# Compact recurrent weights on row halves, and the expert squares on ScalarE, in a one-core TTT, attention and mixture-of-experts kernel

## The reference

```python
def step(carry, xi):                      # per chunk of 128 tokens, 4 heads of 64
    W0, W1, W2, M0, M1, M2 = carry
    qi, ki, vi, l0, l1, l2, mi = xi
    hid = einsum('bcd,bhd->bch', qi, W2)
    gate = silu(einsum('bcd,bhd->bch', qi, W0))
    out = einsum('bch,boh->bco', gate * hid, W1)
    gba = einsum('bcd,bhd->bch', ki, W0)
    hbm = einsum('bcd,bhd->bch', ki, W2)
    sg = silu(gba)
    hidden = sg * hbm
    dhidden = einsum('bco,boh->bch', vi, W1)
    dhbm = dhidden * sg
    dgba = _silu_bp(dhidden * hbm, gba)
    dw1 = einsum('bco,bch->boh', vi, hidden * l1)
    dw0 = einsum('bch,bcd->bhd', dgba, ki * l0)
    dw2 = einsum('bch,bcd->bhd', dhbm, ki * l2)
    ...                                   # momentum, then five Newton-Schulz steps on each
    return (renorm(W0 + dw0, n0), renorm(W1 + dw1, n1), renorm(W2 + dw2, n2), M0n, M1n, M2n), out

# routed experts, 32 of them, latent size 128, weights cw per token
h = square(relu(einsum('tl,eil->eti', x_lat, w1)))
y_lat = einsum('eti,eli->tl', h * cw.T[:, :, None], w2)
```

## Time and profile before

| | |
|---|---|
| median of 3 runs | 830.14 us (828.5 to 830.5) |
| the profiled execution | 830.14 us, of which the span from first to last instruction is 828.1 us |
| TensorE busy | 780.7 us |
| VectorE busy | 714.6 us |
| GpSimd busy | 406.8 us |
| ScalarE busy | 354.0 us |
| relus of the experts on ScalarE | 128, 594 ns each |
| squares of the experts on GpSimd | 128, 1071 ns each |

### The profile page before, as it was taken

One profiled execution on the slowest core, in us unless ns is written; L12 is line 12 of the kernel. 1 busy time (PEld: TensorE's weight loads), 2 busy tenths in 40 slices (PEclk: granted clock), 3 DMA queues, 4 the chain that ended last, 5 costly groups with the idle time before them and its releaser, 6 DMA issues.

```text
span 828.1 us, 24889 instructions
## 1 busy us (share of the span) xinstructions
PE 780.7 (94%) x9776; PEld 668.5 (81%) x9776; DVE 714.6 (86%) x2592; ACT 354.0 (43%) x868; POOL 406.8 (49%) x535
## 2 busy tenths in 40 slices
PE   3899999999999999999999999999999999999997
PEld 1888888888888888878888788887888888888886
DVE  4789898898988979889798897988979889898876
ACT  2544344443444434444344444444444444434533
POOL 1654555445454454544555445544465444655442
PEclk9899999999999999999999999999999999999999
DMA  8100000000000000000000000000000000000000
GB/s 321 54 3 14 9 2 21 3 13 9 2 21 2 14 8 2 21 2 15 8 3 20 2 15 9 3 21 2 15 8 2 21 2 15 8 2 15 2 15 7
DMA packets 9811, 15.09 MB, mean 18 GB/s; under 512 B 1120, under 2 KB 8928, under 8 KB 9440
## 3 DMA queue, kind: packets, MB, share of 16 engines
q1 hardware_dynamic: 7904, 7.80, 3.2%
q10 hardware_dynamic: 1792, 5.70, 1.8%
HBM read 11.41 MB, written 2.10 MB: 16 GB/s over the span
## 4 chain that ended last, share of the span: by engine, by line
PE 53%; DVE 33%; issue 6%; ACT 5%; POOL 2%; DMA 1%; SPq 0%; DVEq 0%
PE CC L629 18%; PE M L629 13%; PE HB L629 8%; DVE acc L1328 8%; PE YB L629 8%; DVE Wn L1175 4%; DVE Mp L1138 2%; DVE dhb L1094 2%; DVE X L1146 2%; PE CC L699 2%; DVE Am L1131 2%; POOL r L285 2%; DVE sm L1233 1%; DMA rows<-in_rows 1%; PE CC L700 1%
## 5 line engine op out<-in xcount | busy, mean ns | idle before, releaser
L363 POOL TENSOR_TENSOR hq<-hr 128x512 f32<-128x512 f32 x128 | 137.1, 1071 | 71.9 <-ACT hr L426 71.9
L285 POOL TENSOR_TENSOR r<-r,half 128x3 f32<-128x3 f32 (+1 forms) x78 | 77.9, 1011 | 155.1 <-DVE r L1116 67.9
L629 PE MATMUL HB<-xlT,e_s 128*128 128x128 f32 x1024 | 143.0, 283 | 0.4 <-ACT xlT L426 0.4
L629 PE MATMUL YB<-e_s,hq 128*128 128x128 f32 x1024 | 141.3, 281 | 1.8 <-DVE acc L1328 0.8
L629 PEld LDWEIGHTS HB<-xlT,e_s 128*128 128x128 f32 x1024 | 126.7, 193 | 6.8 <-ACT xlT L426 0.7
L1328 DVE SCALAR_TENSOR_TENSOR acc<-YB,cw,acc 128x128 f32<-128x128 f32 x448 | 125.4, 342 | 7.9 <-PE YB L629 7.9
L341 POOL TENSOR_TENSOR aX<-X,a_tile 128x192 f32<-128x192 f32 x150 | 92.9, 640 | 79.9 <-DVE X L1146 79.9
L426 ACT ACTIVATE hr<-HB 128x512 f32<-128x512 f32 x128 | 76.1, 594 | 128.5 <-PE HB L629 128.5
L629 PEld LDWEIGHTS YB<-e_s,hq 128*128 128x128 f32 x1024 | 124.2, 191 | 7.4 <-issue 4.1
L629 PEld LDWEIGHTS CC<-X,Mp 64*64 64x64 f32 x1800 | 58.3, 135 | 23.6 <-issue 11.3
L629 PEld LDWEIGHTS CC<-Am 64*64 64x64 f32 x1800 | 59.5, 134 | 21.8 <-DVE Am L1131 18.2
(11 more groups left out here) (180 smaller groups left out, 1525.3 us busy)
## 6 DMA issues: line engine op xcount, KB each, us to landing
xa<-in_x SPq DMA_DIRECT2D x16, 128.0 KB, 2.1
e_s<-in_e1T ACTq DMA_DIRECT2D x1, 2048.0 KB, 12.7
e_s<-in_e2T ACTq DMA_DIRECT2D x1, 2048.0 KB, 19.3
xr<-in_x SPq DMA_DIRECT2D x16, 128.0 KB, 2.2
out<-ot SPq DMA_DIRECT2D x16, 128.0 KB, 1.7
wall<-in_wall SPq DMA_DIRECT2D x1, 820.0 KB, 7.1
up_s<-in_upT ACTq DMA_DIRECT2D x1, 512.0 KB, 15.9
down_s<-in_downT ACTq DMA_DIRECT2D x1, 512.0 KB, 20.0
```

What stands on the lines that cost most here:

```text
L285: return pool.tensor_tensor(dst, src, expo[:, 0:n], ALU.pow)
L363: pool.tensor_tensor(hq[b][:, :, :], hr[b][:, :, :], hr[b][:, :, :], ALU.mult).then_inc(e_hq, 1)
L629: return pe.matmul(out_, lhsT, rhs, start=start, stop=stop)
```

## The change

Two things are changed together. The squares of the experts' rows move from GpSimd (`h_sq`, removed) into `h_relu` on ScalarE; the wait for `y_down(i, u-2)` moves with them and stands ahead of the Relu. The turned weights WT become compact, [128, 3, 64], with head h on partitions 64h to 64h+63: `turn_w` makes them by products with a 64x64 identity on the diagonal quarters, `w_T` copies them by one instruction, `k_side` and `q_side` work on one row half of the array per head, and the k side of head 0 goes to bank CA, that of head 1 to CB. A block-diagonal WO of the third turned weight, for `q_out`, is copied by VectorE in `w_out` behind the k side, in place of W1BD behind `renorm`.

```diff
-            def h_sq(i, u):
-                pool.wait_ge(e_hr, NU * i + u + 1)
-                if u > 1 or not (isinstance(i, int) and i == 0):
-                    pool.wait_ge(e_y, NU * i + u - 1)
-                b = u % 2
-                pool.tensor_tensor(hq[b][:, :, :], hr[b][:, :, :], hr[b][:, :, :], ALU.mult).then_inc(e_hq, 1)
...
             def k_side(i, g):
                 act.wait_ge(e_k[g], i + 1)
-                a(ks[g][:, 0, :], CB[g][:, 0:P], ACT.Sigmoid)
-                a(ks[g][:, 1:3, :].rearrange("p w c -> p (w c)"), CB[g][:, P:3 * P], ACT.Copy).then_inc(e_kc[g], 1)
+                a(ks[g][:, 0, :].rearrange("p (h c) -> p h c", h=2), KS[g][:, :, 0:HD], ACT.Sigmoid)
+                a(ks[g][:, 1:3, :].rearrange("p w (h c) -> p h w c", h=2),
+                  KS[g][:, :, HD:3 * HD].rearrange("p h (w c) -> p h w c", w=2), ACT.Copy).then_inc(e_kc[g], 1)
...
             def w_T(m, g):
 
                 act.wait_ge(e_wt[g], m + 1)
-                for h in range(2):
-                    c = slice(h * HD, (h + 1) * HD)
-                    ins = a(WT[g][c, :, c], CA[g][0:HD, 0:3 * P].rearrange("p (w c) -> p w c", w=3)[:, :, c], ACT.Copy)
-                ins.then_inc(e_WT[g], 1)
+                a(WT[g][:, :, :].rearrange("p w c -> p (w c)"), CA[g][:, 0:3 * HD], ACT.Copy).then_inc(e_WT[g], 1)
...
                 act.wait_ge(e_h, NU * i + u + 1)
                 if u > 1 or not (isinstance(i, int) and i == 0):
                     act.wait_ge(e_hq, NU * i + u - 1)
-                a(hr[u % 2][:, :, :].rearrange("p s t -> p (s t)"), HB[:, :], ACT.Relu).then_inc(e_hr, 1)
+                    act.wait_ge(e_y, NU * i + u - 1)
+                flat = "p s t -> p (s t)"
+                a(hr[u % 2][:, :, :].rearrange(flat), HB[:, :], ACT.Relu).then_inc(e_hr, 1)
+                act.wait_ge(e_hr, NU * i + u + 1)
+                a(hq[u % 2][:, :, :].rearrange(flat), hr[u % 2][:, :, :].rearrange(flat), ACT.Square).then_inc(e_hq, 1)
...
                 pe.wait_ge(e_WT[g], i + 1)
-                mm(CB[g][:, 0:2 * P], qkT[:, 2 + g, :], WT[g][:, W0:W2 + 1, :].rearrange("p w c -> p (w c)"))
-                pe.wait_ge(e_bd[g], i + 1)
-                mm(CB[g][:, 2 * P:3 * P], vT[:, g, :], W1BD[g][:, :]).then_inc(e_k[g], 1)
+                halves = [(slice(h * HD, (h + 1) * HD), (CA, CB)[h][g]) for h in range(2)]
+                for c, dst in halves:
+                    mm(dst[:, 0:2 * HD], qkT[c, 2 + g, :], WT[g][c, W0:W2 + 1, :].rearrange("p w c -> p (w c)"))
+                for c, dst in halves:
+                    ins = mm(dst[:, 2 * HD:3 * HD], vT[c, g, :], Wn[g][c, W1, :])
+                ins.then_inc(e_k[g], 1)
...
                 for w in range(3):
-                    ins = pe.transpose(CA[g][0:HD, w * P:(w + 1) * P], Wn[g][:, w, :], ident[:, :])
+                    for h in range(2):
+                        c = slice(h * HD, (h + 1) * HD)
+                        ins = mm(CA[g][c, w * HD:(w + 1) * HD], Wn[g][c, w, :], ident[c, c])
                 ins.then_inc(e_wt[g], 1)
...
                     for n, w in enumerate((W0, W2)):
-                        ins = mm(M0[:, (2 * g + n) * P:(2 * g + n + 1) * P], WT[g][:, w, :], qkT[:, g, :])
+                        for h in range(2):
+                            c = slice(h * HD, (h + 1) * HD)
+                            ins = mm(M0[c, (2 * g + n) * P:(2 * g + n + 1) * P], WT[g][c, w, :], qkT[c, g, :])
                 ins.then_inc(e_qs, 1)
...
                 for g in range(G):
-                    ins = mm(M1[:, g * P:(g + 1) * P], gh[:, g, :], WT[g][:, W1, :])
+                    pe.wait_ge(e_wo[g], i + 1)
+                    ins = mm(M1[:, g * P:(g + 1) * P], gh[:, g, :], WO[g][:, :])
                 ins.then_inc(e_qo, 1)
...
+            def w_out(i):
+
+                for g in range(G):
+                    dve.wait_ge(e_WT[g], i + 1)
+                    nc.vector.tensor_copy(WO[g][0:HD, 0:HD], WT[g][0:HD, W1, :])
+                    nc.vector.tensor_copy(WO[g][HD:P, HD:P], WT[g][HD:P, W1, :]).then_inc(e_wo[g], 1)
...
                 k_side(i)
+                w_out(i)
                 q_gate(i)
```

More of the change, by code:

```diff
@@ L110, in build @@
         Wn = [sb(f"Wn{g}", [P, 3, HD]) for g in range(G)]
-        W1BD = [sb(f"W1BD{g}", [P, P]) for g in range(G)]
-        WT = [sb(f"WT{g}", [P, 3, P]) for g in range(G)]
+        WT = [sb(f"WT{g}", [P, 3, HD]) for g in range(G)]
+        WO = [sb(f"WO{g}", [P, P]) for g in range(G)]
         Mom = [sb(f"Mom{g}", [P, 3, HD]) for g in range(G)]
@@ L199, in build @@
         CB = [CC[g][:, 512:1024] for g in range(G)]
+        KS = [CC[g][:, :].rearrange("p (h c) -> p h c", h=2)[:, :, 0:3 * HD] for g in range(G)]
         M0 = bank("M0")
@@ L223, in build @@
         e_prod, e_mp = (per_group(n) for n in ("product", "Mp"))
-        e_up, e_rn, e_rp, e_wn, e_bd, e_wt, e_WT = (per_group(n) for n in ("upd", "rn", "rp", "Wn", "W1BD", "wt", "WT"))
+        e_up, e_rn, e_rp, e_wn, e_wo, e_wt, e_WT = (per_group(n) for n in ("upd", "rn", "rp", "Wn", "WO", "wt", "WT"))
         e_qs, e_gsig, e_gt1, e_gh, e_qo, e_to = (sem(n) for n in ("q_side", "gate_sig", "gt1", "gh", "q_out", "to_copied"))
@@ L356, in shared_sq @@
                 pool.tensor_tensor(us[:, :, :], ur[:, :, :], ur[:, :, :], ALU.mult).then_inc(e_us, 1)
-            def h_sq(i, u):
-                pool.wait_ge(e_hr, NU * i + u + 1)
-                if u > 1 or not (isinstance(i, int) and i == 0):
-                    pool.wait_ge(e_y, NU * i + u - 1)
-                b = u % 2
-                pool.tensor_tensor(hq[b][:, :, :], hr[b][:, :, :], hr[b][:, :, :], ALU.mult).then_inc(e_hq, 1)
             def body(i, last):
                 if last:
-                    h_sq(i, 1)
-                    h_sq(i, 2)
                     shared_sq(i)
-                    h_sq(i, 3)
                     rms_pow(i)
-                    for u in range(4, NU):
-                        h_sq(i, u)
                     return
@@ L382, in body @@
                 prep_rstd(m)
[L383 to L386, removed]
+                fill = {0: [lambda: shared_sq(i)], 3: [lambda: rms_pow(i)],
+                        9: [lambda: prep_n8(m)], 16: [lambda: window(m, first)],
                         17: [lambda: prep_kl(m)]}
@@ L397, in body @@
                     row_pow(m, g)
-                h_sq(m, 0)
             prep_rstd(0)
@@ L405, in _ @@
             prep_kl(0)
-            h_sq(0, 0)
             body(0, False)
@@ L978, in _ @@
                 nc.vector.memset(Mom[g][:, :, :], 0.0)
-                nc.vector.memset(W1BD[g][:, :], 0.0)
-                nc.vector.memset(WT[g][:, :, :], 0.0)
+                nc.vector.memset(WO[g][:, :], 0.0)
             nc.vector.memset(lt[:, :, :], 0.0).then_inc(e_init, 1)
@@ L1074, in silu @@
                     dve.wait_ge(e_kc[g], i + 1)
-                    tt(kt[g][:, 0, :], CB[g][:, 0:P], sg[g], ALU.mult).then_inc(e_kd[g], 1)
+                    tt(kt[g][:, 0, :].rearrange("p (h c) -> p h c", h=2), KS[g][:, :, 0:HD],
+                       sg[g].rearrange("p (h c) -> p h c", h=2), ALU.mult).then_inc(e_kd[g], 1)
                 def slope(g):
@@ L1177, in renorm @@
                     ins.then_inc(e_wn[g], 1)
-            def w_bd(m):
+            def w_out(i):
                 for g in range(G):
[L1182 to L1187, removed]
+                    dve.wait_ge(e_WT[g], i + 1)
+                    nc.vector.tensor_copy(WO[g][0:HD, 0:HD], WT[g][0:HD, W1, :])
+                    nc.vector.tensor_copy(WO[g][HD:P, HD:P], WT[g][HD:P, W1, :]).then_inc(e_wo[g], 1)
             def q_gate(i):
@@ L1388, in body @@
                 renorm(m)
-                w_bd(m)
                 total(i)
@@ L1401, in _ @@
                 nc.vector.tensor_copy(nrm[g][:, :], r3[g][:, 4, :]).then_inc(e_up[g], 2)
-            w_bd(0)
             dve.wait_ge(e_const, 16 * NCONST)
```

## The result

The changed kernel takes 930.09 us (928.43 to 930.32), the kernel before 830.32 us beside it: a ratio of 1.120, 95% interval 1.118 to 1.122. It is 100 us slower, 24 us more than the 906 us of the forecast and just inside its range of 875 to 931 us. The profiled execution has a span of 927.9 us.

What follows compares the result with a forecast made beforehand. TensorE, 94% busy, bounds the kernel, under 2.1 us per tile to win. 5.38 - 0.3 - 0.1 = 5.0 us over 15 tiles is 75, plus 0.5 to 1 ahead of tile 0, on 828.1: about 904, plus 2.0 outside the span: 906 us, range 875 to 931.

Steps and rivals of the forecast that it cites:

- Part 1: Squares on ScalarE, their wait on the expert matmul two units back ahead of the Relu: costs 5.38 us per tile.
- The steps: Stalls from the Relu's wait at units 3 to 6: +1.47, +1.90, +1.63 (then +0.30 at a later YB), +0.49 us.
- the +0.08: At unit 5, the XT matmuls behind the sgs matmul come another 0.08 us later.
- step a): Unit 3: Relu waits for YB, then Square and XT copy; first XT matmul 1.47 us later.
- 0.49 given back: The unit 6 stall is taken in by 0.51 us idle before the X,Mp matmuls, where VectorE is late: -0.49 us.
- stall d): Unit 6: Relu, Square, table load, lt and XT copy in a row; XT matmuls 0.49 us later.
- the clock: Rival: each tile has one stretch of 7 us at half speed, 53 us in all, 959 us; chance 7%.
- Part 2: GpSimd no longer holds dhb (0.7 us of TensorE's waits), Wn (0.5) and one lt operation (0.1), per tile.
- Part 3: Compact weights, from Wn to the moments: cost 0.9 us per tile on TensorE, from +0.3 to +2.3.
- overlapping end: Row halves of the array work at once: q side 0.90 us, k side 0.33 per group, +0.3 us in sum.
- The faster one: Rival: waits on e_y already met, squares cost some 0.8 us per tile against 2.1 of old waits; 810 us; chance 4%.
- half hidden: Rival: other old slack takes in the unit 4 or unit 5 stall, 3 us per tile, 875 us; chance 7%.

Runs made afterwards that it cites:

- e5: The changed kernel with matmuls that nobody reads put into TensorE's three long stalls; 906.6 us, ratio 1.0918.
- e1: The changed kernel with four hq buffers instead of two, the Relu waiting for the expert matmul four units back; 828.75 us, ratio 0.9974.
- e7: The changed kernel with four hq buffers, only the Relu of unit 4 still waiting two units back; 865.83 us, ratio 1.0429.
- e8: The changed kernel with four hq buffers, only the Relu of unit 3 still waiting two units back; 848.27 us, ratio 1.0210.
- e4: The kernel before with the squares on ScalarE and four hq buffers, weights as before; 824.48 us, ratio 0.9926.
- e10: The kernel before with the experts' squares left out, YB fed by the Relu from four hr buffers; 799.06 us, ratio 0.9612.
- e12: e11 with compact weights, the WO copies moved behind the reduction of the moments and the two sum copies; 804.3 us, ratio 0.9685.
- e11: e4 with the squares of units 3, 5 and 1 behind the copies that TensorE waits for; 801.43 us, ratio 0.9641.
- e9: The changed kernel, two hq buffers, with the wait on e_y between Relu and Square instead of ahead of the Relu; 868.0 us, ratio 1.0436.

## Why the prediction was right, and what it missed

**Part 1, the wait ahead of the Relu**, was the point, and right in mechanism, place and size. The steps forecast 1.47, 1.90, 1.63 with 0.30 behind it, and 0.49; TensorE's waits at these places are 1.48, 1.81, 1.55, 0.33 and 0.45 us, and by the cuts (table, changed less before) xt0 takes +1.55, wall +1.98, sgs +3.37, of which 1.55 are the half clock and 1.82 the stall (e5), and xt3 +0.87 for the +0.30, the +0.49 and the +0.08. e1 takes the wait away and all of the loss with it; e7 and e8 give single steps, 1.98 and 1.22 us, where the square alone already costs 0.33 of step a) in e1. The reason for the 0.49 given back is wrong, though. At mp 0.71 went (4.39 to 3.68), but mp is 3.67 in e1, e4 and e10 too, which have no stall d): what went there is GpSimd's hold on gs and lt (e10), of which the forecast had 0.1 only.

**The sum** came to 906 us, and the kernel without falls of the clock (e5) takes 906.6 us. That it is so near is partly luck: the stalls cost 6.23 us per tile in e5 where the steps had 5.87 (1.47 + 1.90 + 1.63 + 0.08 + 0.30 + 0.49), and 1.04 came back where 0.89 were taken. What failed is that the clock stood as a rival with 7% and not in the sum. A granted clock under 1 inside the loop was even named as a sign of being wrong, and it came. That 930.09 us is still inside the range, by 1 us, is luck: its upper end of 931 came from the bounds of the other terms, up to 6.7 us per tile, and held nothing for the clock. The size of that rival was off too: it had 7 us at half speed per tile, 53 us in all, from the stretch at 20 to 27 us; it is one fall of 3.4 us in most tiles, 16 of them, 23.5 us. In the forecast I argued that the matmuls around each gap are dense. The row that spoke against it stood in the earlier trace rows: a stretch with 2.00 of 4 us busy came before the fall at 20 us, and around the stall of 1.81 us TensorE is busy 1.49 of 3.30 us.

**Part 2, GpSimd's hold on VectorE**, was right in kind, with one place missed (gs, above): the 30 dhb of the changed kernel last 275 to 280 ns, the Wn 303 to 316, against 1124 and 1035 at the most. Without the squares on GpSimd 2.1 us per tile go (e10), as much as the waits of the earlier trace rows that the prediction had named as the ceiling; place by place the two differ (0.72 at mp for a wait of 0.5, 0.50 from wn0 to q for one of 0.86). The rule of the Trainium skill that was quoted for it, page "SBUF — State Buffer", section "Who interferes with whom", fits the rows of dhb and gs. A Wn multiplication reads one tensor, and of that the rule as quoted says nothing.

**Part 3, the compact weights**, was forecast to cost 0.9 us on TensorE from +0.3 to +2.3, and together with Part 2 to leave -0.3 between the last HB and the next turn of X. Measured: -0.40 there (12.85 before and 12.45 after, the sum of the last nine columns with wn0 taken in), and 0.21 us per tile alone (e12 against e11). So the halves overlap. The k side of the changed kernel, then its q side:

```profile
435.00 0.49 PE L615 MATMUL CC<-WT,qkT 64*128 64x128 f32 x4
435.29 0.37 PE L615 MATMUL CC<-Wn,vT 64*128 64x64 f32 x4
435.48 0.49 PE L615 MATMUL CC<-WT,qkT 64*128 64x128 f32 x4
...
436.07 1.09 PE L615 MATMUL M<-qkT,WT 64*64 64x128 f32 x16
437.09 0.66 PE L758 MATMUL M<-ident,raw 128*128 128x128 f32 x4
```

0.48 us for the first group against 0.67, and 1.02 us for the q side against 0.90: the q side is near its overlapping end of 0.90 and far from the serial 1.79, the k side lies between the 0.33 and the serial end. That end was put at 0.86 without its working; by 0.112 for 128 columns and half of it for 64 it is 0.67. The forecast total of -0.3 was met at -0.40 because two errors cancel. By the table GpSimd's relief in this stretch is 1.35 us (e10 against before; 1.2 forecast). The square in front of the WT copies costs 0.67 (e4 against e10, ks), where nothing was taken. The compact weights with their WO copies cost 0.28 (e1 against e4), where 0.9 were taken; the 0.65 us by which the WO copies delay the sums and X (e12) are in it, and were taken as covered.

**The rivals.** The faster one needed the four stalls together under 2.1 us; TensorE's waits at them are 5.3. Nothing was half hidden. That relief alone can be worth 2.1 us per tile was right. The case that the faster rival described, with the waits on e_y already met, is e1, and it takes 828.75 and not 810 us: the squares also stand in front of the WT copies and of sq, and the compact weights cost. Only with the squares behind these copies (e11 and e12) is 810 us undercut.

## What to carry to other kernels

When a step moves to another engine, look first at the waits that move with it, and ask what stands behind them in the new queue: here the reuse of a double buffer, harmless on an engine that could wait, cost 100 us on one that feeds TensorE, and with two more buffers all of it was gone. An operation that is in nobody's way goes behind the copies that the busiest engine waits for, not in front of them (23 us here). And new stalls of the size seen here (1.5 to 1.8 us) on TensorE are to be priced twice, once as the wait (78 us here) and once as the half clock that can follow it (23.5 us).

## What the runs showed of the hardware that was not expected

The granted clock can fall in a loop that is dense apart from its gaps: TensorE waits of 1.48, 1.81 and 1.55 us per tile brought 16 falls to 1.2 GHz of 3.4 us each, and filling them with unread matmuls that leave 0.62, 0.52 and 0.26 us of waiting brought none. Gaps of 0.77, 1.10 and 0.84 us brought none either (e9). A single gap of about 1.8 us per tile brought 5 falls in 15 tiles (e7), a single one of about 1.5 us brought 1 (e8), so a fall does not belong to a gap with certainty. What decides whether a given gap brings one was not tried.

GpSimd's square holds up even the smallest VectorE operations: gs, on 4 columns, has a median of 653 ns in the kernel before and of 154 ns in e10, and one of the lt, on 12 columns, 383 against 166 ns. A list that looks only at VectorE's large instructions misses them.

TensorE's two row halves work at the same time also when each writes all 128 output partitions, into different PSUM banks: 4 instructions of 128 columns in 0.29 us (435.00 to 435.29), less than 0.112 us each. The Trainium skill, page "TensorEngine Tiling (Array Packing)", section "Theoretical Speedup", has up to 2x; with 0.073 us each against 0.112 this trace shows 1.5x for this form, including the small loss on the way in.
